# A transformer layer with experts: the inverse root of the variance, one power on GpSimd replaced by an integer first guess on VectorE and three Newton rounds on GpSimd

## What is computed

```python
x = L0_attn_x                                   # 8 batches x 512 tokens x 256 features, fp32
x = x + _layernorm(_L0_attn_ref(_layernorm(x), wq, bq, wkv, bkv, wo))       # 16 heads, 4 groups of keys
x = x + _layernorm(_L0_ffn_ref(_layernorm(x), gate_w, w_gate, w_up, w_down, # 64 experts, top 6 of a token,
                               sh_gate, sh_up, sh_down))                    # and a shared expert
# _layernorm(x) = (x - mean) / sqrt(var + 1e-5), over the 256 features
```

## Time and profile before

| what | value |
|---|---|
| time, median of 3 runs | 1541.59 us (1541.21 to 1543.17) |
| the profiled execution: time, span of its instructions | 1543.17 us, 1541.2 us |
| busy, share of the span: PE, PEld, DVE, ACT, POOL | 89%, 76%, 69%, 55%, 51% |
| granted TensorE clock, mean | 0.933 |
| PE's busy share from 208 to 1096 us (six windows of 148 us) | 100% |
| start and end: attention / experts / final stage | 0 to about 1254 / 1288 to 1482 / 1482 to 1541 us |

### The profile page before, as it was taken

The page is one execution under the profiler, slowest core; times in us unless marked ns, Lnnn a source line. Parts: engine busy times, 40 slices in busy tenths (PEclk is TensorE's granted clock), DMA queues, the critical chain, the costliest instruction groups (busy, mean ns, idle before and its releaser), DMA issues.

```text
span 1541.2 us, 25400 instructions
## 1 busy us (share of the span) xinstructions
PE 1364.1 (89%) x8322; PEld 1167.8 (76%) x8322; DVE 1058.1 (69%) x3444; ACT 846.2 (55%) x2267; POOL 778.6 (51%) x1022
## 2 busy tenths in 40 slices
PE   4899999999999999999999999999999956767610
PEld 3788889888988898889888988898889843333300
DVE  4867686888688878886888688868886854111117
ACT  4666665666566666666666566666666612222204
POOL 1555564556454645564556455646564412444543
PEclk9899999999999999999999999999999967686865
DMA  8100000100100010001000100010000582999664
GB/s 284 38 1 1 15 15 15 33 14 15 32 28 1 15 39 22 1 15 38 22 1 15 39 22 1 15 39 22 1 15 25 142 231 76 232 238 233 154 188 155
DMA packets 94993, 95.75 MB, mean 62 GB/s; under 512 B 6065, under 2 KB 87314, under 8 KB 94866
## 3 DMA queue, kind: packets, MB, share of 16 engines
q1 hardware_dynamic: 88722, 84.70, 18.3%
q0 software_dynamic: 6144, 9.44, 3.3%
HBM read 67.78 MB, written 26.35 MB: 61 GB/s over the span
## 4 chain that ended last, share of the span: by engine, by line
PE 78%; DMA 6%; issue 5%; DVE 5%; POOL 3%; ACT 1%; SPq 1%; POOLq 0%; ACTq 0%; DVEq 0%
PE bank_s L519 17%; PE bank_t L519 17%; PE bank_o L519 15%; PE bank_y L519 12%; PE bank_f L519 7%; DMA ffn_sums<-dsum,idx_s 5%; PE bank_s L599 4%; PE bank_t L599 3%; PE bank_f L599 2%; POOL ffn_sums L1545 1%; POOL xg L1534 1%; DVE fstat L1059 1%; DMA fb<-ffn_sums 1%; DVE fa L1405 0%; PE bank_t L532 0%
## 5 line engine op out<-in xcount | busy, mean ns | idle before, releaser
L1455 POOL TENSOR_TENSOR prob<-prob,rinv 128x512 f32<-128x512 f32 (+3 forms) x512 | 366.9, 725 | 216.9 <-DVE rinv L1149 216.7
L857 ACT ACTIVATE prob<-prob,negmax 128x512 f32<-128x512 f32 (+3 forms) x512 | 285.4, 558 | 60.7 <-DVE negmax L1142 59.9
L1442 POOL TENSOR_TENSOR q_l<-q_sum,q_h 128x128 fp32r<-128x128 f32 (+1 forms) x256 | 184.1, 740 | 150.8 <-ACT q_h L837 148.9
L519 PE MATMUL bank_o<-pt_h,v_h 128*128 128x128 f32 (+3 forms) x512 | 168.9, 330 | 0.0
L519 PE MATMUL bank_o<-pt_h,v_l 128*128 128x128 f32 (+3 forms) x512 | 164.9, 322 | 0.0
L519 PE MATMUL bank_o<-pt_l,v_h 128*128 128x128 f32 (+3 forms) x512 | 164.0, 320 | 0.0
L866 ACT ACTIVATE pt_h<-bank_s 128x128 fp32r<-128x128 f32 (+3 forms) x214 | 93.3, 436 | 89.2 <-PE bank_s L599 71.1
L1142 DVE CUSTOM_DVE_ANT_0 prob<-bank_t,causal 128x384 f32<-128x384 f32 (+3 forms) x226 | 110.5, 489 | 27.8 <-PE bank_t L519 27.2
L1142 DVE CUSTOM_DVE_ANT_0 prob<-bank_s,causal 128x512 f32<-128x512 f32 (+3 forms) x217 | 107.9, 497 | 26.9 <-PE bank_s L519 25.9
L837 ACT ACTIVATE q_h<-q_sum 128x512 fp32r<-128x512 f32 x128 | 80.2, 627 | 66.6 <-DVE q_sum L1119 66.6
L519 PE MATMUL bank_y<-o_h,wo_h 128*128 128x512 f32 x256 | 112.5, 440 | 2.7 <-DVE o_l L1160 2.7
(11 more groups left out here) (342 smaller groups left out, 4193.6 us busy)
## 6 DMA issues: line engine op xcount, KB each, us to landing
w_gu<-in_w_gate SPq DMA_DIRECT2D x64, 176.0 KB
w_gu<-in_w_up SPq DMA_DIRECT2D x64, 176.0 KB
w_dn<-in_w_down SPq DMA_DIRECT2D x64, 176.0 KB
xio<-in_x SPq DMA_DIRECT2D x16, 512.0 KB, 4.0
token_table<-rows SPq DMA_DIRECT2D x8, 640.0 KB, 3.7
ffn_sums<-keys SPq DMA_DIRECT2D x4, 1024.0 KB
x_rows<-xio SPq DMA_DIRECT2D x8, 512.0 KB, 2.9
ffn_sums<-ytr SPq DMA_DIRECT2D x16, 256.0 KB, 2.1
```

The costliest lines, as they stand in the source:

```text
L519: return pe.matmul(o, l, r, start=start, stop=stop, skip_group_check=True)
L857: act.activation(p_, p_, ACT.Exp, bias=negmax[:, r, i:i + 1], scale=-1.0, accum_out=rsum[:, r, i:i + 1]).then_inc(exp_made, 1)
L1442: pool.tensor_tensor(l_[:, cols], q_sum[:, cols], plain(h_)[:, cols], ALU.subtract).then_inc(pos_low, 1)
L1455: pool.tensor_tensor(p_, p_, rinv[:, r, i:i + 1].to_broadcast([P, (i + 1) * P]), ALU.mult).then_inc(prob_made, 1)
```

## The change

EPS is added on DVE, which also makes an integer first guess y = MAGIC - (v >> 1) on the bits of the variance, each of these small operations waiting for the one before it. POOL refines y by three Newton rounds y = y (1.5 - 0.5 v y y), of four operations each, all waiting for the one before. `inv_made` comes behind the third round. In the loop the three rounds have places of their own in `QUIET`; at the start, for the last batch and in the final stage they follow each other. `nw` holds v, y and a scratch row (four rows instead of one). In the final stage the bias is made by POOL in two operations instead of by DVE in one, and DVE no longer waits there for `inv_made`.

```diff
         QUIET = {
-            (2, 3): ("stat1",), (3, 3): ("norm1",), (4, 1): ("stat2",), (5, 0): ("norm2",), (11, 1): ("statx",),
-            (12, 1): ("normx",)}
+            (2, 3): ("stat1", 0), (3, 0): ("stat1", 1), (3, 1): ("stat1", 2), (3, 3): ("norm1",),
+            (4, 1): ("stat2", 0), (4, 2): ("stat2", 1), (4, 3): ("stat2", 2), (5, 0): ("norm2",),
+            (11, 1): ("statx", 0), (11, 2): ("statx", 1), (11, 3): ("statx", 2), (12, 1): ("normx",)}
...
 # DVE, variance()
                 for i in range(n):
                     last = dve.bn_aggr(mvt[:, i, :], statt[:, i, :])
-                last.then_inc(var_made, 1)
+                done(last)
+                v, y, a = (nwt[:, q, 0:n] for q in range(3))
+                done(dve.tensor_scalar(v, mvt[:, 0:n, 1:2].rearrange("p i o -> p (i o)"), EPS, None, ALU.add))
+                done(dve.tensor_scalar(a.bitcast(I32), v.bitcast(I32), 1, None, ALU.logical_shift_right))
+                dve.tensor_scalar(y.bitcast(I32), a.bitcast(I32), -1.0, float(MAGIC), ALU.mult, ALU.add
+                                  ).then_inc(var_made, 1)
...
 # DVE, quiet(): only the first of the three steps of a statistic does anything
+                if step[2:] and step[2]:
+                    return
...
 # DVE, final stage
-                dve.wait_ge(inv_made, len(VARS) + p + 1)
-                dve.scalar_tensor_tensor(out=fnw[p % 2][:, 1, :], in0=fmv[p % 2][:, :, 0:1].rearrange("p i o -> p (i o)"),
-                                         scalar=-1.0, in1=fnw[p % 2][:, 0, :], op0=ALU.mult, op1=ALU.mult
-                                         ).then_inc(bias_made, 1)
...
 # POOL
+            def newton(nwt, n, r):
+                v, y, a = (nwt[:, q, 0:n] for q in range(3))
+                if r == 0:
+                    variances[0] += 1
+                    pool.wait_ge(var_made, variances[0])
+                done(pool.tensor_tensor(a, y, y, ALU.mult))
+                done(pool.tensor_tensor(a, a, v, ALU.mult))
+                done(pool.tensor_scalar(a, a, -0.5, 1.5, ALU.mult, ALU.add))
+                last = pool.tensor_tensor(y, a, y, ALU.mult)
+                if r < 2:
+                    done(last)
+                else:
+                    last.then_inc(inv_made, 1)
...
-            def inverse_root(mvt, nwt, n):
-                variances[0] += 1
-                pool.wait_ge(var_made, variances[0])
-                y = nwt[:, 0, 0:n]
-                done(pool.tensor_scalar(y, mvt[:, 0:n, 1:2].rearrange("p i o -> p (i o)"), EPS, None, ALU.add))
-                pool.tensor_tensor(y, y, minus_half[:, 0:n], ALU.pow).then_inc(inv_made, 1)
...
 # POOL, start and last batch: each inverse_root(mv, nw, TT) becomes
+            for r in range(3):
+                newton(nw, TT, r)
...
 # POOL, final stage
-                inverse_root(fmv[p % 2], fnw[p % 2], 2 * TT)
+                for r in range(3):
+                    newton(nwt, 2 * TT, r)
+                pool.wait_ge(inv_made, variances[0])
+                done(pool.tensor_tensor(nwt[:, 3, :], fmv[p % 2][:, :, 0:1].rearrange("p i o -> p (i o)"),
+                                        nwt[:, 1, :], ALU.mult))
+                pool.tensor_scalar(nwt[:, 3, :], nwt[:, 3, :], -1.0, None, ALU.mult).then_inc(bias_made, 1)
```

More of the change, by code:

```diff
@@ L18 @@
 EPS = 1e-5
+MAGIC = 0x5F3759DF
 BIG = 3.0e38
@@ L135, in build @@
         mv = place("mv", [P, TT, 2], F32)
-        nw = place("nw", [P, 1, TT], F32)
-        minus_half = place("minus_half", [P, 2 * TT], F32)
+        nw = place("nw", [P, 4, TT], F32)
         zero_f = keys[:, CAP:CAP + ROW]
@@ L182, in build @@
         fmv = [place(f"fmv{i}", [P, 2 * TT, 2], F32) for i in range(2)]
-        fnw = [place(f"fnw{i}", [P, 2, 2 * TT], F32) for i in range(2)]
+        fnw = [place(f"fnw{i}", [P, 4, 2 * TT], F32) for i in range(2)]
         fb = [place(f"fb{i}", [P, TT, E], F32) for i in range(2)]
@@ L1035, in scalar_program @@
                     last = act.activation(fa[b][:, k, :], fa[b][:, k, :], ACT.Identity,
-                                          scale=nw_[:, 0, k0 + k:k0 + k + 1], bias=nw_[:, 1, k0 + k:k0 + k + 1])
+                                          scale=nw_[:, 1, k0 + k:k0 + k + 1], bias=nw_[:, 3, k0 + k:k0 + k + 1])
                 last.then_inc(final_normed, 1)
@@ L1495, in gpsimd_program @@
             pool.memset(zero_f, 0.0).then_inc(zero_made, 1)
-            done(pool.memset(minus_half[:], -0.5))
-            inverse_root(mv, nw, TT)
+            for r in range(3):
+                newton(nw, TT, r)
             pool.wait_ge(consts_made, 1)
@@ L1566, in gpsimd_program @@
                         add_sums(b)
+                nwt = fnw[p % 2]
                 if p > 1:
                     pool.wait_ge(final_normed, 2 * p - 2)
-                inverse_root(fmv[p % 2], fnw[p % 2], 2 * TT)
+                for r in range(3):
+                    newton(nwt, 2 * TT, r)
[3 more added lines that the diff above has]
+                pool.tensor_scalar(nwt[:, 3, :], nwt[:, 3, :], -1.0, None, ALU.mult).then_inc(bias_made, 1)
         block = ctx.enter_context(nc.Block())
```

4 lines of the change are left out of this document (2 added, 2 removed).

## The result

| | before | after |
|---|---|---|
| median, us | 1541.90 (1541.21 to 1543.17) | 1570.64 (1566.18 to 1572.91) |
| the profiled execution: time, span, us | 1543.17, 1541.2 | 1569.09, 1567.3 |

The medians of the table are 28.7 us apart. The ratio on record is 1.0169 (95% interval 1.0143 to 1.0195), or 26.1 us; over all 21 executions of the changed kernel on record with it the median is 1567.56 us. The median of the table lies 9.6 us above the range of 1545 to 1561.

The account below looks back on a forecast made before the run. PE was taken to bound attention, with the statistics themselves the path at the start, last batch and final stage. 5.8 + 1.05 + 0 + 1.0 = 7.85 us gave 1549.4 us against the median, 0.5% slower; range 1545 to 1561.

Parts of the forecast that it names:

- the loop, +1.0 us: Seven batches of three statistics: 0.15 us per batch for the first statistic, nothing for the others, +1 us in all.
- one margin, that of `prob` for the transposes of head 3: Loop, behind the y statistic: POOL finished piece 3 1.48 us before PE's transpose; the rounds take the whole margin.
- The hold-up of the earlier trace: Final stage: L1420 on DVE took 1.77 us instead of 0.17 while POOL added sums, one engine holding up the other.
- rival D: Loop loses more, by dearer DVE operations or DVE blocking POOL: +3.5 to +10 more, 1553 to 1560 us; chance 0.17.
- Rival A: Small POOL operations dear, 410 ns each, at start, last batch, final stage and loop: +31, 1572.5 us; chance 0.10.
- The end of the last batch: Gathering to normalisation 4.36 us instead of 1.47, 2.89 more for each of y and x2, nothing hidden: +5.8 us.
- PE's wait for x2: Sign at the end of the last batch: PE's wait for x2, 12.8 us before, would be near 18.6 us.
- The start: First normalisation at 13.84 instead of 12.79, as the longer chain outgrows the cover of DVE's splits: +1.05 us.
- The final stage: DVE's dropped wait against a longer POOL chain held up by DVE's residuals: between -4.5 and +2.1 us, taken as 0.

Follow-up runs that it names:

- before, x norm earlier: Kernel before the change, with the normalisation of x moved from head 12, phase 1 to phase 0; 1543.85 us, ratio 1.0017.
- POOL's half, norms later: Changed kernel without the added DVE operations, constant first guess, normalisations of x and x2 moved later; 1548.27 us, a single execution.
- DVE's half: Changed kernel with EPS and guess still on DVE, but one power on POOL instead of the Newton rounds; 1538.44 us, ratio 0.9993.
- x and x2 later: Changed kernel with normalisation of x at head 13, phase 1, x2 at head 5, phase 1, and neighbouring work moved; 1557.48 us, ratio 1.0093.
- x later: Changed kernel with the normalisation of x moved from head 12 to head 13, phase 1; 1557.38 us, ratio 1.0101.
- POOL's half: Changed kernel without the three DVE operations; POOL adds EPS and makes three rounds from a constant first guess of 1; 1556.4 us, ratio 1.010.
- DVE's half doubled: Changed kernel with POOL's power instead of rounds, plus three further small DVE operations (the shift repeated) per statistic; 1559.04 us, ratio 1.0106.
- rounds together: Changed kernel with the three rounds of a statistic made one after the other in the power's old place; 1585.99 us, ratio 1.0304.
- The new order alone: Kernel before the change with only the final stage reordered: POOL makes the bias behind the power, DVE doesn't wait; 1530.63 us, ratio 0.9939.

## Why the prediction was wrong

**One account for the loop.** Take as DVE's extra time in the loop what the normalisations took beyond 33.7 us, DVE's idle time ahead of them, and the added small operations with their gaps (14.2 to 14.5 us, 26.9 when doubled), against what the loop lost:

| kernel | DVE's extra time | loop |
|---|---|---|
| before, x norm earlier | 4.3 | +4.2 |
| POOL's half, norms later | 9.9 | +3.3 |
| DVE's half | 14.2 | +6.8 |
| x and x2 later | 9.0 + 14.4 = 23.4 | +12.1 |
| x later | 10.2 + 14.5 = 24.7 | +15.5 |
| POOL's half | 19.0 + 5.0 = 24.0 | +15.7 |
| DVE's half doubled | 26.9 | +19.0 |
| changed kernel | 17.6 + 0.6 + 14.2 = 32.4 | +22.6 |
| rounds together | 7.6 + 14.2 = 21.8 | +38.6, and PE waits 16.4 for `prob` |

All but the first and the last lose 7 to 11 us less than DVE's extra time, some 0.3 to 0.5 us a statistic; the first loses all of it. I read this as the slack that DVE has there, beyond which its time is PE's time. It is a reading of seven loops that holds within some 4 us, not a law: the slack differs from place to place. In the last row late `prob` comes on top, and the terms named there still leave 7 us or more of the 38.6 open.

**The step that failed is the loop, +1.0 us against 22.6.** It had two parts. "DVE has 0.6 us more, three times a batch, and waits enough in between" priced DVE at nothing. DVE does wait in the loop, but too little at the places of the statistics: DVE's half alone cost +6.8. And the rounds were priced by one margin, that of `prob` for the transposes of head 3. That count held: PE waited 0.2 to 0.3 us a batch for `prob` there. What I left out was whom POOL's delayed work would meet. The hold-up of the earlier trace rows, 1.77 us against 0.17, was used for the final stage and in rival D as 0.5 to 1.5 us a batch, but not for DVE's normalisations. POOL's half alone cost +15.7. Rival D came nearest, since in it the two engines hold each other up in the loop, but the other way round: DVE stops POOL's rounds, and PE waits for `prob` of head 3. It priced that at 4.5 to 11 us with the forecast's 1, at most half of what was lost. Rival A came near the time, 1572.5, by a mechanism that didn't happen: the small operation costs 0.20 us.

**The end of the last batch** was right in kind: 2.53 us for each of the two statistics instead of 2.89, because an operation is 0.28 from start to start, not 0.31. PE's wait for x2 is 17.8 us, 18.6 was said.

**The start** came 2.2 us later than before instead of 1.05. The chain did outgrow its cover, but a term is missing: it was itself stretched where it ran beside DVE's splits, which have two SBUF inputs. Four of its operations took 0.51 to 0.66 us instead of 0.20, 1.4 us more in all, and it ended 4.7 us after its start instead of the 3.64 of the prediction. The hold-up of the earlier trace rows was left out here as it was in the loop. The first weights landed 1.16 us later in this execution (the table load on ACT, which waits for them, began at 9.58 instead of 8.42), but that isn't the cause: in the other execution of the changed kernel it began at 8.33, and the normalisation at 14.84 all the same, against 14.96 here. The timeline of after, in order of time:

```profile
11.35 0.20 POOL L1448 TENSOR_TENSOR nw<-nw 128x4 f32<-128x4 f32 x1
11.53 2.50 DVE L1053 SCALAR_TENSOR_TENSOR wkv_l<-stage,wkv_h 128x512 fp32r<-128x512 f32 x4 [1.40 <-ACT wkv_h L828]
11.62 0.66 POOL L1449 TENSOR_TENSOR nw<-nw 128x4 f32<-128x4 f32 x1
12.37 0.51 POOL L1450 TENSOR_SCALAR nw<-nw 128x4 f32<-128x4 f32 x1
12.97 0.52 POOL L1451 TENSOR_TENSOR nw<-nw 128x4 f32<-128x4 f32 x1
13.56 0.52 POOL L1448 TENSOR_TENSOR nw<-nw 128x4 f32<-128x4 f32 x1
14.17 0.20 POOL L1449 TENSOR_TENSOR nw<-nw 128x4 f32<-128x4 f32 x1
```

**The final stage**, 0 against -0.8 us, has the two halves that were named, a gain by the order and a loss by the longer chains and their meetings. That they cancel so closely was in part luck, since the prediction only bounded the stage between -4.5 and +2.1 us and took 0. The new order alone is worth 8.9 us; the rounds and their meetings eat most of it. The prediction's 0.2 us for each of DVE's operations didn't hold here either: in the second and third pair the shift (L1067) took 1.73 us beside POOL's sums (L1572), and 0.17 in the others. In the last pair, after (the whole of it answers to the earlier trace rows):

```profile
1554.44 1.23 DVE L1413 TENSOR_TENSOR fa<-fa,fx 128x1024 f32<-128x1024 f32 x1 [1.71 <-ACT fa L1036]
1554.58 1.15 POOL L1450 TENSOR_SCALAR fnw<-fnw 128x8 f32<-128x8 f32 x1
...
1556.41 1.24 DVE L1413 TENSOR_TENSOR fa<-fa,fx 128x1024 f32<-128x1024 f32 x1 [0.74 <-ACT fa L1036]
1556.65 1.05 POOL L1450 TENSOR_SCALAR fnw<-fnw 128x8 f32<-128x8 f32 x1
```

Each of these residuals stops one small operation of POOL for nearly its own length (1.15 and 1.05 us instead of 0.20). The Trainium skill (SBUF — State Buffer, section "SBUF: two separate sides") says that the one that started first keeps the shared pair for its whole instruction and that the other fully blocks; these rows agree. The same section counts among the holders a VectorE operation in a mode that uses both ports, without a second input.

Whether DVE's normalisations behave so can be read from their durations. The view of one line of DVE gives duration in ns as minimum, median and maximum, first before, then after the change:

```profile
L1075 DVE TENSOR_SCALAR xio<-xio,mv,nw x28: 398/404/659, 139.1 to 1048.5; 128x256 f32<-128x256 f32 x28
L1081 DVE TENSOR_SCALAR xio<-xio,mv,nw x28: 484/613/1103, 142.3 to 1071.6; 128x256 f32<-128x256 f32 x28
```

In the single records of the changed kernel, 70 of the 84 normalisations started beside a running POOL instruction, and each of the 70 ended 0.15 us after that instruction did, however long it had still to run. The other 14 took 0.40 us. Before the change 34 of the 84 met one. So its end hangs on the end of POOL's instruction and not on its own work, which fits the page's rule. POOL's own pieces were hardly longer beside them (1060 ns for a `q_l` of 384 columns, 1014 elsewhere). And not every DVE instruction is stopped: making `pt_l` of 384 columns, with one of its inputs in PSUM, took 553 ns under POOL's work and 552 without it, and the partial statistics, which read 256 columns from SBUF, 414 ns in both cases. So what is held is not all of DVE's way to SBUF. That it is the port pair is the page's word, and no run here separates it from another shared resource; the runs show which instructions are held up, beside what and how long.

What stays open: how much of the y share (16.9 us of normalisation instead of 12.6) can be had back, since moving y's normalisation moves the whole chain behind it and wasn't tried.

## What to carry to other kernels

When work is added to an engine that has idle time, ask where its later instructions will lie, and what its other work would hold up there. A margin to the final consumer isn't enough. An engine that shows waits all through a loop can still have no slack at the one place where work is added: three operations of 0.2 us cost half their time, the next three nearly all of it. And take a wait out before the work behind it: in the kernel before, making the bias on POOL, so that DVE doesn't wait for the inverse root in the final stage, was worth 8.9 us by itself.

## What the runs showed of the hardware beyond that

A power on POOL took 1.04 us at 128x4, against 0.20 us for a multiplication of the same size, and one round of four dependent operations 1.05 us (1268.72 to 1269.77 in the timeline of after), about the same. In the profile of PE, waits showed only half of what this loop lost. The starts of a named instruction, compared head by head, show all of it: between the kernel before and the one with the bias on POOL, whose loops are alike, they agree within 0.02 us over 128 heads, and between the two executions of the changed kernel within 0.5.
